# A recurrence in two chains of eight images in place of one chain of sixteen

## The chip, the cores and the metric

The kernel runs on one core of a Trainium2 chip. Its engines are PE (TensorE: matmuls, with its weight loads shown apart as PEld), DVE (VectorE), ACT (ScalarE), POOL (GpSimd) and SP (SyncE, which issues the DMAs). Each has its own stream of instructions, and they meet at semaphores. The metric is the time of one execution on the device in microseconds. Before the change it is 4371.48 us, the median of 3 runs (4370.07 to 4373.3).

## What is computed

The input x has 16 images of 64 channels and 36 x 100 pixels, f32. Four layers follow, each on a normalised x and added to x: sweeps of convolutions, a routed feed-forward layer, sweeps again, and last a recurrence over the 3600 pixels of an image. Only the last layer is touched:

```python
def _L1_ffn_ref(x, W, V, gamma, beta):        # x: (16, 3600, 64) tokens
    Wx = jnp.einsum('bti,hi->bth', x, W)      # then batch norm with gamma, beta
    ...
    Vt = V.T
    def step(yt, wx_t):
        yt = jax.nn.sigmoid(wx_t + yt @ Vt)
        return (yt, yt)
    y0 = jnp.zeros((B, H), dtype=Wx.dtype)
    _, ys = jax.lax.scan(step, y0, jnp.swapaxes(Wx, 0, 1))
    return jnp.swapaxes(ys, 0, 1)
```

Each of the 3600 steps needs the result of the one before. The 16 images don't depend on one another.

## The kernel before

The earlier stages take the first 2475 us or so: norms, which multiply blocks of 400 tokens (L560, L568), sweeps of convolutions, where PE works through L742 and L764, and the routed layer. The last norm leaves the normalised tokens of all images in the buffer `img`. From there the recurrence runs to the end, and every engine has its own loop for it.

The 3600 steps are cut into segments of SEG = 30 steps, and BODY = 4 segments make one iteration of the loops of ACT, DVE and SP (NIT = 30 of them). PE's loop takes 2 segments at a time, 60 iterations. PSUM holds the input part (wx_t) of a segment, 16 columns a step, in bank s for segments of kind s (even or odd).

- PE, for each step (L921 to L944): it waits until the last sigmoid has been counted in `step_y`, multiplies the state before (`yb`, 65 rows, 16 columns) by `vt` in two matmuls of 32 outputs each (L932), adding to what the bank holds, and counts in `step_mm`. In the first 12 steps of a segment it then makes one twelfth of the next segment's input part, `fill_input` (L822 to L829), two matmuls of 40 columns from a staged buffer, and multiplies 512 columns of zeros (`keep_clock`, L832). In the other 18 steps it multiplies 512 and 256 columns of zeros. An f32 matmul stands in the trace as two weight loads and two matmuls. At a segment's first step it also counts in `seg_done`, in every second one it clears `step_y`, and it waits for `staged`.
- ACT, for each step (L1141 to L1146): it waits for `step_mm`, applies the sigmoid to 16 columns of PSUM and writes them to `yb`, and counts in `step_y`. At a segment's first step it also waits for `added`; every 120 steps it clears `step_mm`.
- DVE (L1416), once a segment: it adds the segment's results to the tokens of x2 that SP has loaded into `x2b`, into `ob`.
- POOL (L472), once a segment: it copies the tokens of the segment after next into a staged buffer.
- SP (L450 to L454), once per 4 segments: it loads `x2b` and stores `ob`, 480 KB each, in runs of 480 bytes.

Order is fixed by each engine's program alone; nothing is scheduled. The semaphore waits of PE and ACT are constants, which is why the counters are cleared.

## Time and profile before

| | us |
|---|---|
| median of 3 runs | 4371.48 |
| the profiled execution | 4369.35 |
| its span in the trace | 4367.6 |
| PE busy in the span | 4235.1 (97%) |
| PEld busy | 2684.2 (61%) |
| ACT busy | 1477.0 (34%) |
| DVE busy | 1321.1 (30%) |

The page cuts the span into 40 slices of 109 us. From slice 23 on PE is busy, PEld and ACT at three tenths each, DVE nearly idle, the DMAs at 18 GB/s or less: that is the recurrence, 43% of the span. Busy time of PE counts the multiplied zeros of `keep_clock` as well. In the timeline an entry is a run of like instructions: when it began, how long it lasted, engine, line, operands, how many, and in brackets how long the engine had been idle before it and whom it waited for. Times in the answers are from the start of the span.

### The profile page before, as it was taken

How to read it: one execution, taken by the hardware profiler on the slowest of the kernel's cores; microseconds unless marked ns; L12 is line 12 of the kernel's file. 1: busy time of each engine (PE TensorE's matmuls, PEld its weight loads, DVE VectorE, ACT ScalarE, POOL GpSimd, SP SyncE). 2: the span in 40 equal slices, each digit the busy share in tenths (PEclk: the TensorE clock that was granted, in tenths of full speed). 3: DMA queues.
4: the chain of work that ended last, by engine and by line, in shares of the span. 5: the costliest groups of instructions: out<-in, count | busy, mean ns of one | idle time of the engine just before them, and what ended most of it. 6: DMA issues, size and time to landing. Idle time of an engine off the chain costs nothing.

```text
span 4367.6 us, 106368 instructions
## 1 busy us (share of the span) xinstructions
PE 4235.1 (97%) x42882; PEld 2684.2 (61%) x42882; DVE 1321.1 (30%) x2468; ACT 1477.0 (34%) x5372; POOL 109.2 (3%) x182
## 2 busy tenths in 40 slices
PE   7999999999889999999998899999999999999999
PEld 2799999994352899999993333333333333333333
DVE  3555533334555655533335500000000000000000
ACT  5002344335545002333444233333333333333333
POOL 1000000000010000000000000000000000000000
PEclk8899999999999999999999899999999999999999
DMA  5000000003348000000007200000000000000000
GB/s 138 15 0 0 0 0 0 0 0 108 97 115 254 16 0 0 0 0 0 0 0 200 66 18 10 17 18 18 9 18 18 18 9 18 18 18 9 18 18 14
DMA packets 146888, 139.19 MB, mean 32 GB/s; under 512 B 79710, under 2 KB 146302, under 8 KB 146814
## 3 DMA queue, kind: packets, MB, share of 16 engines
q1 hardware_dynamic: 146814, 138.21, 12.3%
q8 instruction: 46, 0.75, 0.1%
q14 instruction: 28, 0.23, 0.0%
HBM read 79.19 MB, written 58.98 MB: 32 GB/s over the span
## 4 chain that ended last, share of the span: by engine, by line
PE 94%; DVE 3%; ACT 1%; issue 1%; SPq 0%; DMA 0%; DVEq 0%; ACTq 0%; PEldq 0%
PE ps L832 23%; PE ps L764 21%; PE ps L742 18%; PE ps L932 17%; PE ps L827 3%; PE ps L568 2%; PE ps L560 1%; PE ps L715 1%; PE ps L579 1%; PE ps L589 1%; PE ps L603 1%; DVE rstd L1160 1%; PE ps L805 1%; PE ps L682 1%; PE ps L633 1%
## 5 line engine op out<-in xcount | busy, mean ns | idle before, releaser
L832 PE MATMUL ps<-idle 128*32 128x512 bf16 (+1 forms) x5894 | 1635.0, 339 | 0.0
L932 PEld LDWEIGHTS ps<-xl,vt 65*32 65x32 f32 x14400 | 520.9, 108 | 1163.3 <-ACT xl L1146 1111.3
L1146 ACT ACTIVATE xl<-ps 64x16 f32<-64x16 f32 x3600 | 637.2, 177 | 1250.9 <-PE ps L932 1250.9
L764 PE MATMUL ps<-xl,taps 128*128 128x128 f32 (+2 forms) x7880 | 921.5, 279 | 4.7 <-DVE xl L1332 4.7
L764 PEld LDWEIGHTS ps<-xl,taps 128*128 128x128 f32 x7880 | 920.8, 191 | 5.7 <-issue 5.3
L932 PE MATMUL ps<-xl,vt 65*32 65x16 f32 x14400 | 871.2, 193 | 7.8
L742 PE MATMUL ps<-split 128*128 128x400 f32 x4140 | 781.3, 352 | 12.8 <-DVE split L1327 12.8
L742 PEld LDWEIGHTS ps<-split 128*128 128x128 f32 x4140 | 779.2, 190 | 16.6 <-issue 15.2
L1416 DVE TENSOR_TENSOR xl<-xl 64x480 f32<-64x480 f32 x120 | 116.5, 971 | 1772.9 <-PEq L929 886.7
L1002 ACT ACTIVATE img<-xl 128x144 f32 x788 | 366.0, 465 | 556.4 <-DVE xl L1309 556.4
L1309 DVE SCALAR_TENSOR_TENSOR xl<-ps,img 128x144 f32<-128x144 f32 x788 | 323.2, 410 | 597.2 <-PE ps L764 597.2
L832 PEld LDWEIGHTS ps<-idle 128*32 128x32 bf16 x5894 | 426.8, 97 | 21.9 <-issue 10.2
L827 PE MATMUL ps<-xl 128*32 128x40 f32 x5808 | 357.1, 204 | 0.3 <-DVE vt L1408 0.3
L968 ACT ACTIVATE xl<-img 64x400 f32 (+1 forms) x68 | 36.6, 539 | 654.6 <-DVE split L1280 654.6
L1294 DVE SCALAR_TENSOR_TENSOR split<-ps,img 128x400 fp32r<-128x400 f32 x276 | 158.5, 574 | 298.9 <-PE ps L742 298.9
L827 PEld LDWEIGHTS ps<-xl 128*32 128x32 f32 x5808 | 219.1, 112 | 0.5 <-DVE vt L1408 0.5
L1280 DVE TENSOR_TENSOR split<-img,split 128x400 fp32r<-128x400 f32 x280 | 161.1, 575 | 37.9 <-DVE split L1324 1.1
L568 PE MATMUL ps<-rstd,spread 32*128 32x400 f32 x576 | 145.5, 582 | 15.9 <-DVE rstd L1160 14.4
L1296 DVE SCALAR_TENSOR_TENSOR img<-ps,img 128x400 f32 x276 | 155.7, 564 | 0.0
L472 POOL COPY xl<-img 128x240 f32 (+1 forms) x121 | 73.9, 612 | 2942.9 <-PE ps L827 1779.0
L568 PEld LDWEIGHTS ps<-rstd,spread 32*128 32x128 f32 x576 | 53.3, 194 | 106.0 <-issue 32.6
L1051 ACT ACTIVATE taps<-ps 128x400 f32<-128x400 f32 x144 | 72.8, 506 | 114.7 <-PE ps L604 74.5
(153 smaller groups left out, 1681.1 us busy)
## 6 DMA issues: line engine op xcount, KB each, us to landing
ring<-in_x_dram SPq DMA_DIRECT2D x144, 200.0 KB, 3.7
x_dram<-sums SPq DMA_DIRECT2D x144, 200.0 KB, 3.3
t_dram<-sums SPq DMA_DIRECT2D x72, 200.0 KB, 3.6
ring<-t_dram SPq DMA_DIRECT2D x72, 200.0 KB, 3.9
ring<-x_dram SPq DMA_DIRECT2D x72, 200.0 KB, 3.7
xl<-x_dram SPq DMA_DIRECT2D x30, 480.0 KB, 6.3
out_dram<-xl SPq DMA_DIRECT2D x30, 480.0 KB, 4.7
img<-in_L_ffn_weight_dram SPq DMA_DIRECT2D x4, 512.0 KB
```

The costliest lines, as they stand in the source:

```text
L568: pe.matmul(PS[bank][:, 0:CH], spread32[32 * q:32 * q + 32, p * 64:p * 64 + 128], rstd[32 * q:32 * q + 32, (g % 2) * CH:(g % 2 + 1) * CH], ...
L742: ins = pe.matmul(acc[:, :, j0:j1], taps_part[tap_part][:, t0:t0 + 128], line_pairs(h, line_part, j0 + d, j1 + d), start=(tap_part == line ...
L764: last = pe.matmul(acc[:, :, lo:hi], taps[:, (k * NO + d + 2) * 128:(k * NO + d + 3) * 128], column[h][:, :, lo + d:hi + d], start=(n == 0 ...
L827: last = pe.matmul(acc[c * 32:(c + 1) * 32, t0:t0 + FILL_T, h * HB:(h + 1) * HB], wsc[1 - h][:, c * 32:(c + 1) * 32], stage[j][:, t0:t0 + ...
L832: pe.matmul(PS[bank][0:32, 0:n], idle[:, 0:32], idle[:, 0:n], start=True, stop=True)
L932: last = pe.matmul(PS[s][c * 32:(c + 1) * 32, t * B:(t + 1) * B], vt[:, c * 32:(c + 1) * 32], prev, start=False, stop=True, skip_group_che ...
L1002: act.activation(column_at(l, h, x), column[h], ACT.Copy).then_inc(put_back[l][h], 1)
L1146: act.activation(yb[0:64, s % 2, :, t], PS[s % 2][0:64, t * B:(t + 1) * B], ACT.Sigmoid).then_inc(step_y, 1)
L1280: dve.tensor_tensor(line_pairs(h, 1), line, line_pairs(h, 0), ALU.subtract).then_inc(lo[l][h], 1)
L1294: dve.scalar_tensor_tensor(out=line_pairs(h, 0), in0=acc, scalar=0.0, in1=line, op0=ALU.max, op1=ALU.add).then_inc(hi[l][h], 1)
L1296: dve.scalar_tensor_tensor(out=line, in0=acc, scalar=0.0, in1=line, op0=ALU.max, op1=ALU.add).then_inc(state[l][h], 1)
L1309: dve.scalar_tensor_tensor(out=column[h], in0=acc, scalar=0.0, in1=column_at(l, h, x), op0=ALU.max, op1=ALU.add).then_inc(state[l][h], 1)
```

## The change

The 16 images become two groups of eight, h = 0 and 1, each a chain of its own with its own counters, `step_y[h][j]` and `step_mm[h][j]`, j for segments of even and odd number. A chain's counter of one kind is cleared at the first step of a segment of the other kind. In each step PE does chain 0's two matmuls (8 columns), then a part of `fill_input` in the first 8 steps of a segment or 256 columns of zeros in the others, then chain 1's two matmuls, then 256 columns of zeros. ACT does two sigmoids of 8 columns. Each chain has its banks: 2s + h, and the zeros go to bank 4. SEG becomes 20: 180 segments, of which PE's loop still takes 2 (90 iterations) and the loops of ACT, DVE and SP 4 (45 iterations, transfers of 320 KB in runs of 320 bytes).

```diff
-SEG = 30
+SEG = 20
...
-            pool.memset(yb[0:64, 1, :, SEG - 1], 0.0).then_inc(step_y, 2 * SEG)
+            for h in range(2):
+                alone(pool.memset(yb[0:64, 1, h * HB:(h + 1) * HB, SEG - 1], 0.0))
+                pool.sem_inc(step_y[h][1], SEG)
...
-            acc = PS[j][0:64, 0:SEG * B].rearrange("p (t b) -> p t b", b=B)
+            acc = PS[2 * j + h][0:64, 0:SEG * HB].rearrange("p (t b) -> p t b", b=HB)
             for c in range(2):
-                last = pe.matmul(acc[c * 32:(c + 1) * 32, t0:t0 + FILL_T, h * HB:(h + 1) * HB], wsc[1 - h][:, c * 32:(c + 1) * 32],
-                                 stage[j][:, t0:t0 + FILL_T, :], start=(part == 0), stop=True, skip_group_check=True)
+                last = pe.matmul(acc[c * 32:(c + 1) * 32, t0:t0 + FILL_T, :], wsc[1 - h][:, c * 32:(c + 1) * 32],
+                                 stage[j][:, t0:t0 + FILL_T, :], start=(t0 == 0), stop=True, skip_group_check=True)
...
-                        n = s * SEG + t
-                        if n == 0:
-                            pe.wait_ge(step_y, 2 * SEG)
-                            pe.sem_clear(step_y)
-                        else:
-                            pe.wait_ge(step_y, n)
-                        if t == 0:
-                            pe.sem_inc(seg_done, 1)
-                        prev = yb[:, s, :, t - 1] if t else yb[:, 1 - s, :, SEG - 1]
-                        for c in range(2):
-                            last = pe.matmul(PS[s][c * 32:(c + 1) * 32, t * B:(t + 1) * B], vt[:, c * 32:(c + 1) * 32],
-                                             prev, start=False, stop=True, skip_group_check=True)
-                        last.then_inc(step_mm, 1)
-                        if t < 2 * FILLS:
+                        for h in range(2):
+                            pe.wait_ge(step_y[h][s] if t else step_y[h][1 - s], t if t else SEG)
+                            images = slice(h * HB, (h + 1) * HB)
+                            prev = yb[:, s, images, t - 1] if t else yb[:, 1 - s, images, SEG - 1]
+                            for c in range(2):
+                                last = pe.matmul(PS[2 * s + h][c * 32:(c + 1) * 32, t * HB:(t + 1) * HB], vt[:, c * 32:(c + 1) * 32],
+                                                 prev, start=False, stop=True, skip_group_check=True)
+                            last.then_inc(step_mm[h][s], 1)
                             if t == 0:
-                                pe.wait_ge(staged, i * 2 + (s + 2))
-                            last = fill_input(pe, 1 - s, t)
-                            if t == 2 * FILLS - 1:
-                                last.then_inc(filled, 1)
-                            keep_clock(pe, 512)
-                        else:
-                            keep_clock(pe, 512)
-                            keep_clock(pe, 256)
+                                pe.sem_clear(step_y[h][1 - s])
+                                if h == 1:
+                                    pe.sem_inc(seg_done, 1)
+                            if h == 0 and t < 2 * FILLS:
+                                if t == 0:
+                                    pe.wait_ge(staged, i * 2 + (s + 2))
+                                last = fill_input(pe, 1 - s, t)
+                                if t == 2 * FILLS - 1:
+                                    last.then_inc(filled, 1)
+                            else:
+                                keep_clock(pe, 256, 4)
...
-                        n = s * SEG + t
-                        act.wait_ge(step_mm, n + 1)
-                        if n == BODY * SEG - 1:
-                            act.sem_clear(step_mm)
-                        act.activation(yb[0:64, s % 2, :, t], PS[s % 2][0:64, t * B:(t + 1) * B], ACT.Sigmoid).then_inc(step_y, 1)
+                        for h in range(2):
+                            act.wait_ge(step_mm[h][s % 2], t + 1)
+                            act.activation(yb[0:64, s % 2, h * HB:(h + 1) * HB, t], PS[s % 2 * 2 + h][0:64, t * HB:(t + 1) * HB], ACT.Sigmoid
+                                           ).then_inc(step_y[h][s % 2], 1)
+                            if t == 0:
+                                act.sem_clear(step_mm[h][1 - s % 2])
```

The rest of the diff makes room for the added semaphores: in the routed layer and the setup, counters that were counted one after another become one (`ffn_tr`, `ffn_taken`, `rnn_w_ready`), with the same waits in the same places.

The order of PE's instructions around a segment boundary in the middle of its loop. L932 (in the new kernel L930) are the matmuls of a step, L827 (L830) those of the input part, L832 (L835) the zeros, ISA the clear. Before:

```order
L932 MATMUL ps<-xl,vt 32x16
L832 MATMUL ps<-idle 32x512
L832 MATMUL ps<-idle 32x256
L932 MATMUL ps<-xl,vt 32x16 [waits step_y]
L932 MATMUL ps<-xl,vt 32x16
L937 REGISTER_ALU
L827 MATMUL ps<-xl 32x5x8 [waits staged]
L827 MATMUL ps<-xl 32x5x8
L832 MATMUL ps<-idle 32x512
```

Now:

```order
L930 MATMUL ps<-xl,vt 32x8 [waits step_y0_0]
L930 MATMUL ps<-xl,vt 32x8
L934 ISA
L939 REGISTER_ALU
L830 MATMUL ps<-xl 32x40 [waits staged]
L830 MATMUL ps<-xl 32x40
L930 MATMUL ps<-xl,vt 32x8 [waits step_y1_0]
L930 MATMUL ps<-xl,vt 32x8
L934 ISA
L835 MATMUL ps<-idle 32x256
```

The clear, the register instruction, the wait for `staged` and the input matmuls now stand between the two chains' matmuls, and the second clear between chain 1's matmuls and its zeros.

The end of PE's loop, where it jumps back. Before:

```order
L932 MATMUL ps<-xl,vt 32x16 [waits step_y]
L932 MATMUL ps<-xl,vt 32x16
L832 MATMUL ps<-idle 32x512
L832 MATMUL ps<-idle 32x256
L919 REGISTER_ALU
L919 COMPARE_AND_BRANCH
```

Now:

```order
L930 MATMUL ps<-xl,vt 32x8 [waits step_y0_1]
L930 MATMUL ps<-xl,vt 32x8
L835 MATMUL ps<-idle 32x256
L930 MATMUL ps<-xl,vt 32x8 [waits step_y1_1]
L930 MATMUL ps<-xl,vt 32x8
L835 MATMUL ps<-idle 32x256
L922 REGISTER_ALU
L922 COMPARE_AND_BRANCH
```

The jump follows on chain 1's matmuls, and what comes behind it is the first step of chain 0.

ACT at a segment boundary, L1146 (now L1145) the sigmoid. Before:

```order
L1146 ACTIVATE xl<-ps 64x16 [waits step_mm] x29
L1140 REGISTER_ALU
L1146 ACTIVATE xl<-ps 64x16 [waits step_mm,added]
```

Now:

```order
L1145 ACTIVATE xl<-ps 64x8 [waits step_mm1_0]
L1141 REGISTER_ALU
L1145 ACTIVATE xl<-ps 64x8 [waits step_mm0_1,added]
L1148 ISA
L1145 ACTIVATE xl<-ps 64x8 [waits step_mm1_1]
L1148 ISA
L1145 ACTIVATE xl<-ps 64x8 [waits step_mm0_1]
```

A clear now follows each chain's first sigmoid of a segment.

## Rows read from the trace of the kernel before

**Rows 1.** Groups by shape, 2477.5 to 4361: count, busy us, mean ns, idle before
```profile
L832 PE MATMUL ps<-idle 128*32 128x512 bf16 x3597 | 1361.6, 379 | 0.0
...
L1146 ACT ACTIVATE xl<-ps 64x16 f32<-64x16 f32 x3595 | 636.4, 177 | 1247.2 <-PE ps L932 1247.2
L832 PE MATMUL ps<-idle 128*32 128x256 bf16 x2159 | 583.0, 270 | 0.0
L932 PEld LDWEIGHTS ps<-xl,vt 65*32 65x32 f32 x14380 | 519.8, 108 | 1162.3 <-ACT xl L1146 1110.3 <-issue 52.0
```
**Rows 2.** Windows: length, busy us and count by engine, granted clock, DMA share, GB/s
```profile
2477.50:4361.00 1883.50, 1875.67 (x25884) 721.21 (x25880) 115.52 (x119) 636.35 (x3595) 72.23 (x118) 1.00 0.07 15
...
1040.00:1070.00 30.00, 24.37 (x213) 17.82 (x215) 19.81 (x20) 16.13 (x26) 3.19 (x1) 0.89 0.00 1
```
**Rows 3.** Timeline of an ordinary step: start, length, what, idle before
```profile
3000.53 0.18 ACT L1146 ACTIVATE xl<-ps 64x16 f32<-64x16 f32 x1 [0.34 <-PE ps L932]
3000.76 0.14 PEld L932 LDWEIGHTS ps<-xl,vt 65*32 65x32 f32 x4 [0.34 <-ACT xl L1146]
...
3000.84 0.48 PE L832 MATMUL ps<-idle 128*32 128x512 bf16 x2
3001.05 0.18 ACT L1146 ACTIVATE xl<-ps 64x16 f32<-64x16 f32 x1 [0.34 <-PE ps L932]
```
**Rows 4.** Timeline, a segment's second step and the next boundary (inside PE's loop)
```profile
2601.87 0.18 ACT L1146 ACTIVATE xl<-ps 64x16 f32<-64x16 f32 x1 [0.34 <-PE ps L932]
...
2616.38 0.18 ACT L1146 ACTIVATE xl<-ps 64x16 f32<-64x16 f32 x1 [0.34 <-PE ps L932]
2616.67 0.17 PEld L932 LDWEIGHTS ps<-xl,vt 65*32 65x32 f32 x4 [0.40 <-issue]
...
2616.84 0.15 PEld L827 LDWEIGHTS ps<-xl 128*32 128x32 f32 x4
...
2617.04 0.18 ACT L1146 ACTIVATE xl<-ps 64x16 f32<-64x16 f32 x1 [0.48 <-PE ps L932]
```
**Rows 5.** Line L1146 alone: count, ns min/median/max, first and last start
```profile
L1146 ACT ACTIVATE xl<-ps x3600: 177/177/178, 2475.2 to 4361.3; 64x16 f32<-64x16 f32 x190
```
**Rows 6.** Timeline of the boundary where PE's and ACT's loops turn
```profile
2600.07 0.18 ACT L1146 ACTIVATE xl<-ps 64x16 f32<-64x16 f32 x1 [0.34 <-PE ps L932]
...
2600.67 0.18 ACT L1146 ACTIVATE xl<-ps 64x16 f32<-64x16 f32 x1 [0.43 <-PE ps L932]
...
2601.00 0.15 PEld L932 LDWEIGHTS ps<-xl,vt 65*32 65x32 f32 x4 [0.52 <-issue]
...
2601.35 0.18 ACT L1146 ACTIVATE xl<-ps 64x16 f32<-64x16 f32 x1 [0.50 <-PE ps L932]
```
**Rows 7.** Lines L1051, L932 and L568 alone, as in rows 5
```profile
L1051 ACT ACTIVATE taps<-ps x144: 503/503/514, 1003.6 to 2439.9; 128x400 f32<-128x400 f32 x144
...
L932 PE MATMUL ps<-xl,vt x14400: 176/183/236, 2474.8 to 4360.9; 65*32 65x16 f32 x198
...
L568 PE MATMUL ps<-rstd,spread x576: 494/598/1032, 46.6 to 2460.6; 32*128 32x400 f32 x192
```
**Rows 8.** Timeline of a step with input matmuls
```profile
3010.24 0.14 PEld L932 LDWEIGHTS ps<-xl,vt 65*32 65x32 f32 x4 [0.28 <-ACT xl L1146]
...
3010.30 0.15 PEld L827 LDWEIGHTS ps<-xl 128*32 128x32 f32 x4
...
3010.40 0.38 PE L832 MATMUL ps<-idle 128*32 128x512 bf16 x1
```
**Rows 9.** Timeline, the last add
```profile
4361.56 0.96 DVE L1416 TENSOR_TENSOR xl<-xl 64x480 f32<-64x480 f32 x1 [14.81 <-PEq L946]
```
**Rows 10.** Timeline, the loop's first steps, granted clock still at the lower level
```profile
2475.18 0.18 ACT L1146 ACTIVATE xl<-ps 64x16 f32<-64x16 f32 x1 [1.89 <-PE ps L932]
...
2475.79 0.18 ACT L1146 ACTIVATE xl<-ps 64x16 f32<-64x16 f32 x1 [0.43 <-PE ps L932]
...
2476.45 0.18 ACT L1146 ACTIVATE xl<-ps 64x16 f32<-64x16 f32 x1 [0.49 <-PE ps L932]
```

More of the change, by code:

```diff
@@ L120, in metaformer @@
         yb = xl[0:65, 0:2 * SEG * B].rearrange("p (s t b) -> p s b t", s=2, b=B)
-        x2b = xl[0:64, 1920:3840].rearrange("p (b t) -> p b t", b=B)
-        ob = xl[0:64, 3840:5760].rearrange("p (b t) -> p b t", b=B)
+        x2b = xl[0:64, 1920:1920 + BODY * SEG * B].rearrange("p (b t) -> p b t", b=B)
+        ob = xl[0:64, 3840:3840 + BODY * SEG * B].rearrange("p (b t) -> p b t", b=B)
         wsc = [xl[:, 5760 + h * 64:5824 + h * 64] for h in range(2)]
@@ L164, in __init__ @@
                     self.summed = sem(f"ln{n}_summed")
+                if n in (1, 2):
                     self.mixed = sem(f"ln{n}_mixed")
@@ L192, in metaformer @@
         xt_tr, xt_kept = sem("xt_tr"), sem("xt_kept")
-        hid_tr, hid_turned, eo_kept, eo_tr = (sem(n) for n in ("hid_tr", "hid_turned", "eo_kept", "eo_tr"))
+        ffn_tr, ffn_taken = sem("ffn_tr"), sem("ffn_taken")
         ew_dma, hid_mm, hid_act, eo_mm, outt_ready, lh_tr, lh_ready = (
@@ L197, in metaformer @@
             sem(n) for n in ("rdma", "rnn_t", "rnn_w_ready", "bn_pe", "bn_dve", "bn_step", "rnn_ready"))
-        bn_std, rnn_t_taken, rnn_c = sem("bn_std"), sem("rnn_t_taken"), sem("rnn_c")
+        bn_std, rnn_c = sem("bn_std"), sem("rnn_c")
         pool_done, taps_blank = sem("pool_done"), sem("taps_blank")
         passed = sem("passed")
-        step_mm, step_y, seg_done, x2_in, added, out_st = (
-            sem(n) for n in ("step_mm", "step_y", "seg_done", "x2_in", "added", "out_st"))
+        step_mm, step_y = ([[sem(f"{n}{h}_{j}") for j in range(2)] for h in range(2)] for n in ("step_mm", "step_y"))
+        seg_done, x2_in, added, out_st = (sem(n) for n in ("seg_done", "x2_in", "added", "out_st"))
         staged, filled = sem("staged"), sem("filled")
@@ L846, in _ @@
             pe.wait_ge(centre_ready, 1)
-            pe.wait_ge(rnn_t_taken, 1)
+            pe.wait_ge(rnn_w_ready, 1)
             for h in range(2):
@@ L875, in _ @@
                     last = pe.transpose(PS[4 + j][:, u * 128:(u + 1) * 128], hidden[:, j * 512 + u * 128:j * 512 + (u + 1) * 128], ident[:, :])
-                last.then_inc(hid_tr, 1)
+                last.then_inc(ffn_tr, 1)
             for part in range(2):
@@ L881, in _ @@
             for j in range(4):
-                pe.wait_ge(hid_turned, j + 1)
+                pe.wait_ge(ffn_taken, j + 1)
                 for e8 in (2 * j, 2 * j + 1):
@@ L889, in _ @@
             last.then_inc(eo_mm, 1)
-            pe.wait_ge(eo_kept, 1)
+            pe.wait_ge(ffn_taken, 5)
             for e8 in range(8):
@@ L893, in _ @@
                 if e8 % 4 == 3:
-                    last.then_inc(eo_tr, 1)
+                    last.then_inc(ffn_tr, 1)
             pe.wait_ge(outt_ready, 2)
@@ L900, in _ @@
             pe_layer(pe, 1)
-            pe.wait_ge(rnn_w_ready, 1)
+            pe.wait_ge(rnn_w_ready, 2)
             pe_token_norm(pe, 3)
@@ L945, in _ @@
-            pe.wait_ge(step_y, 2 * SEG)
+                        for h in range(2):
[6 more added lines that the diff above has]
+                            last.then_inc(step_mm[h][s], 1)
+                            if t == 0:
+                                pe.sem_clear(step_y[h][1 - s])
[9 more added lines that the diff above has]
+                                keep_clock(pe, 256, 4)
@@ L946, in _ @@
+            for h in range(2):
+                pe.wait_ge(step_y[h][1], SEG)
             pe.sem_inc(seg_done, 1)
@@ L1141, in _ @@
                     for t in range(SEG):
-                        n = s * SEG + t
-                        act.wait_ge(step_mm, n + 1)
-                        if n == BODY * SEG - 1:
-                            act.sem_clear(step_mm)
-                        act.activation(yb[0:64, s % 2, :, t], PS[s % 2][0:64, t * B:(t + 1) * B], ACT.Sigmoid).then_inc(step_y, 1)
+                        for h in range(2):
+                            act.wait_ge(step_mm[h][s % 2], t + 1)
[3 more added lines that the diff above has]
+                                act.sem_clear(step_mm[h][1 - s % 2])
         def dve_taps(dve, l):
@@ L1359, in _ @@
                 dve.tensor_copy(half(wbd, h)[:, h * 64:(h + 1) * 64], PS[7][0:64, 64:128])
-            dve.tensor_copy(vt[0:64, :], PS[7][0:64, 128:192]).then_inc(rnn_t_taken, 1)
+            dve.tensor_copy(vt[0:64, :], PS[7][0:64, 128:192]).then_inc(rnn_w_ready, 1)
             dve_taps(dve, 0)
@@ L1372, in _ @@
             for j in range(4):
-                dve.wait_ge(hid_tr, j + 1)
-                dve.tensor_copy(hidden_t[:, j * 512:(j + 1) * 512], PS[4 + j][:, :]).then_inc(hid_turned, 1)
+                dve.wait_ge(ffn_tr, j + 1)
+                dve.tensor_copy(hidden_t[:, j * 512:(j + 1) * 512], PS[4 + j][:, :]).then_inc(ffn_taken, 1)
             dve.wait_ge(eo_mm, 1)
-            dve.tensor_copy(mixed_out, PS[0][:, :]).then_inc(eo_kept, 1)
+            dve.tensor_copy(mixed_out, PS[0][:, :]).then_inc(ffn_taken, 1)
             for u in range(2):
-                dve.wait_ge(eo_tr, u + 1)
+                dve.wait_ge(ffn_tr, 5 + u)
                 dve.tensor_copy(outt.rearrange("p (b a x) -> p b a x", a=4, x=8)[:, :, :, 4 * u:4 * u + 4],
```

## The prediction, written before the result was known

> **What bounds the kernel now.** The page's slices and groups point at one loop, from 2477 to 4361 us; I then read its groups by shape, stretches by window, and the timeline of single steps. In the loop stand 14380 small weight loads of L932, 3595 sigmoids of L1146, and the idle matmuls of L832 [rows 1]. TensorE looks full there (1875.67 us busy of 1883.50, at a granted clock of 1.00) [rows 2], but the reader is to see what it is full of: L832 multiplies zeros, to keep the clock up. The loop is a closed chain of 3600 steps, two matmuls then one sigmoid that feeds the next two. The timeline shows one turn of it [rows 3]: the weight load of L932 starts 0.23 us after the sigmoid started (0.18 of it the sigmoid, 0.05 the way back), the next sigmoid starts 0.29 us after that load. ACT's idle gap of 0.34 and PE's of 0.34 are both waits for the other. So the loop is bound by latency, and by no engine's rate.
>
> Its size: from the sigmoid at 2601.87 to that at 2616.38 [rows 4] are 28 steps without a boundary, 14.51/28 = 0.5182 us each. All 3600 sigmoids start between 2475.2 and 4361.3 [rows 5], 1886.1 us. 3599 x 0.5182 is 1865.0, so 21.1 us are extras: 119 segment boundaries of about 0.15 (2616.38 to 2617.04 is 0.66 [rows 4], and 0.67 in the other kind [rows 6], for 0.52), 30 turns of ACT's loop of about 0.08 (2600.07 to 2600.67 is 0.60 [rows 6]), and 0.4 us of steps at the lower clock at the start.
>
> **What two chains can and can't do.** A chain's next step still waits for its own sigmoid, so two chains don't halve the step. Both advance once per turn of one chain, and a turn gets shorter only by what 8 images cost less than 16. Everything else is a question of whether the second chain fits into the gaps of the first.
>
> **Term 1, shorter operations.** The sigmoid reads 16 columns in 177 ns, L1051 reads 400 from PSUM in 503 [rows 7]: (503 - 177)/384 = 0.85 ns a column, so 8 fewer give 6.8 ns. For the matmul the nearest pair is L932's 183 ns for 16 f32 columns and the shortest of L568, 494 ns for 400 [rows 7]: 0.81 ns a column, 6.5 ns for 8. Only the last of the matmuls counts, those before it hide behind the next weight load. Together 13.3 ns, a turn of 0.505 us, and 3600 x 13.3 ns = 47.9 us. The lower bound is the sigmoid's part alone, 24 us; the upper is a matmul part half as long again, 60 us.
> A rule of the Trainium skill speaks against the matmul half. "TensorE: Matmul & The Clock Gate", section "Back-to-back issue gap", says that starts of matmuls never come closer than about 25 ns however few columns they have; by it the term would be 24 us only. No row here has 8 columns, so the trace doesn't decide it; I take the slope because what counts here is the end of one matmul and not the distance between two.
>
> **Term 2, does the second chain fit?** On PE a group (matmuls plus filler) took, in a step with input matmuls, from the load at 3010.24 over that of L827 at 3010.30 to the filler's start at 3010.40 [rows 8], 0.16 us. The new order has that without the filler in chain 0, and in chain 1 (and in both where no input is made) the matmuls, 0.08 us to the filler's start [rows 3], and 256 columns of filler, 0.11 us (a filler of 512 columns is recorded with 379 ns, one of 256 with 270) [rows 1]: 0.19 us. Two groups need 0.35 to 0.38 of 0.505 us, so each chain finds PE free if they stand 0.19 to 0.31 apart. ACT needs 2 x 0.17 = 0.34 of 0.505. I cost ordinary steps at nothing beyond term 1; the cover is 0.12 us a step on PE, and if it is gone the turn grows one for one.
>
> **Term 3, boundaries: 180 for 120.** Before, at a boundary, the load of L932 comes 0.29 after the sigmoid's start instead of 0.23 (the wait and the count of seg_done stand alone in front of it), and the next sigmoid 0.37 after it instead of 0.29 (two waits, `added` too) [rows 4]. In the new order the matmul waits itself and the clear and count come after it, so the 0.06 goes, and some 0.03 of slower loading (0.17 for 0.14, the length of the two load rows [rows 3, 4]); about 0.05 for the second wait on ACT stays. What is new lies between the two chains. On PE the clear, the register instruction and the wait on `staged` stand between chain 0's matmuls and chain 1's: register and wait cost 0.11 (0.17 from load to input load for 0.06 in an ordinary step [rows 4, 8]), the clear about 0.10 (0.33 from sigmoid to load for 0.29 with a plain count, and that 0.06 over none [rows 4, 6]). Chain 1's load can then start 0.06 + 0.11 + 0.10 + 0.06 = 0.33 us after chain 0's; it was due 0.25 after, a delay of 0.08. Chain 1's own clear pushes its filler to end about 0.63, where chain 0 is due at 0.585. ACT's two clears (0.08 each by [rows 6]) stand between sigmoids that are 0.25 apart, with 0.08 to spare, and cost nothing. DVE's add and the pool's copy, for whom the counts of seg_done and filled are, have some 10 us and keep it. In all 0.05 to 0.15 a boundary; I take 0.075, 13.5 us.
>
> **Term 4, PE's loop turns: 90 for 60.** Before, PE jumps while it would wait for the sigmoid anyway. From the last load before the turn (0.23 after 2600.07) to the first behind it (2601.00) are 0.70 us [rows 6], and the jump, the register instructions and a clear fit in there. In the new order the last group is chain 1's, chain 0 is due only about 0.26 us later, and nothing covers the rest. The price is above 0 (if the jump is short) and below 0.70 - 0.26 = 0.44 us a turn. No row shows the jump alone; I take 0.2, the middle: 18 us, with 0 and 40 as ends. The Trainium skill ("Advanced Engine Details and Errata", section "Control Flow Timing") gives about 108 ns for a compare-and-branch and 51 ns for a branch; by that alone the turn would cost nothing or little, and the sum would be some 15 us lower; no row here shows it.
>
> **Term 5, the ends.** From DVE's last add at 4361.56 [rows 9] to the end of the span, 4367.6, it is one add and one store; both shrink by a third in size, and a good part of each is fixed: -1 us. Four input parts fewer ahead of the loop: below 1 us. Merged semaphores of the earlier stages keep the same order of waits: 0. Packets of 320 bytes for 480, in 45 for 30 transfers each way: hidden, since x2's load has a segment (10 us) to land.
>
> **Sum.** Terms 3 and 4 give 31.5 us (9 to 67) in place of 21.1: +10. With -48 and -1 that is -39 us. The profiled execution took 4369.35 us (span 4367.6 and 1.75 around it), 2.1 below the median of 4371.48; on the median's side 4332.5.
>
> **Rivals.**
> (A) The forecast: 4333 us, its own range 4300 to 4362 by the bounds of the terms. 0.55.
> (B) The matmul's part doesn't shrink, or the chains touch by some 7 ns a step: 4371.5 - 24 + 10 - 1 = 4356. For it: PE's loads of 32 columns (0.14 us for four [rows 3]) are as long as before. 0.13.
> (C) Turns and boundaries at their upper ends: 67 for 21.1 is +46, with a gain of 24 to 48 that gives 4369 to 4392. For it: PE's order is now shared, and a late chain passes its lateness on. 0.10.
> (D) The other side: the clock. Zeros are multiplied in 768 columns a step now (512 with input matmuls); then it is 512, and 256 with input matmuls, in a turn that is hardly shorter. Where PE waited more, as at 1040 to 1070, the granted clock falls (0.89, with PE busy 24.37 of 30 us) [rows 2]. At the lower of its two levels, 1.2 GHz, the first steps of this loop took 0.61 and 0.66 us (2475.18, 2475.79, 2476.45) [rows 10] for 0.518: at least 0.09 us a step. All 3600 so would be +324 us, 4657; the input steps alone (8 of 20) +130, 4463. It turns the sign from 39/0.09 = 430 steps on, 12% of them. Against it: the loop now runs at 1.00 for 1883 us with a steady pattern [rows 2], the new pattern has no long gap either, and four weight loads more a step. 0.20, the price anywhere from 4380 to 4660.
> (E) The change doing nothing of what it says is excluded by the order of instructions, which has the two chains; 0.02 for what I don't see.
>
> **How the numbers follow.** The likeliest is 4333. The range must hold A, B and most of C: 4298 (term 1 at 60, terms 3 and 4 low) to 4388 leaves out D and the rest, 0.2. A measurement of this kernel can tell about 0.2% (9 us) from no change: faster, below 4362.7, is A and B, 0.68; within 0.2% is half of C and a little of D, 0.09; slower is the rest, 0.23.
>
> **What would show it.** Sigmoids of 170 ns, in pairs; those of one chain 0.505 apart within a segment, the second about 0.25 behind the first. If 0.512, B. The stretch of the loop at a granted clock of 1.00; anything lower is D and outweighs all other terms. Intervals of 0.58 at boundaries of one chain, and of about 0.8 at every second one, where PE turns; if the latter are 0.6, term 4 was too dear. PE's idle time before L932 should be `issue` at turns only. Wrong in its ground would be an ordinary turn above 0.518, for then the chains hinder each other in every step.

## The result, and the profile after

The changed kernel takes 4342.36 us (median of 4 runs, 4336.4 to 4347.19) against 4370.77 (4368.68 to 4373.3) for the kernel before, measured beside it: a ratio of 0.9933, interval 0.9921 to 0.9945. It is faster by 28.4 us, which is three times what a measurement can tell. The forecast was 4333 with the sign right and 9 us too little. The profiled execution took 4347.19 us (span 4345.4), the slowest of the four. The runs lie in two pairs, about 4347 and about 4337. The account below is that of one run of the slower pair, and the gap of 10 us is taken up in the part on the prediction.

The groups of the loop in the page after (columns as in [rows 1], with the mean over all shapes):

```profile
L930 PE MATMUL ps<-xl,vt 65*32 65x8 f32 x28800 | 1700.5, 187 | 9.5
L1145 ACT ACTIVATE xl<-ps 64x8 f32<-64x8 f32 x7200 | 1224.3, 170 | 638.1 <-PE ps L930 44.7
L930 PEld LDWEIGHTS ps<-xl,vt 65*32 65x32 f32 x28800 | 1059.5, 108 | 627.6 <-ACT xl L1145 26.7
```

There are twice as many sigmoids, each 170 ns for 177, and four weight loads a chain and step. The line L1145 alone answers to [rows 5]:

```profile
L1145 ACT ACTIVATE xl<-ps x7200: 170/170/173, 2479.6 to 4340.5; 64x8 f32<-64x8 f32 x195
```

The sigmoids span 1860.9 us for 1886.1 before: 25.2 us less. What else differs lies outside: the loop begins at 2479.6 for 2475.2, though nothing that costs time was changed ahead of it. In the traces of all fourteen kernels here that point lies between 2470.8 and 2485.3 with the same stages ahead of it, so these 4 us are within its scatter. Behind the last sigmoid stand 4.9 us for 6.3.

An ordinary stretch in the timeline of after (columns as in [rows 3]):

```profile
3000.02 0.14 PEld L930 LDWEIGHTS ps<-xl,vt 65*32 65x32 f32 x4
...
3000.28 0.14 PEld L930 LDWEIGHTS ps<-xl,vt 65*32 65x32 f32 x4
3000.28 0.23 PE L930 MATMUL ps<-xl,vt 65*32 65x8 f32 x4
...
3000.53 0.14 PEld L930 LDWEIGHTS ps<-xl,vt 65*32 65x32 f32 x4
```

One chain loads at 3000.02 and 3000.53, the other at 3000.28, in the middle. And the boundary where PE's loop turns, which answers to [rows 6]:

```profile
3119.85 0.14 PEld L930 LDWEIGHTS ps<-xl,vt 65*32 65x32 f32 x4
...
3120.08 0.14 PEld L930 LDWEIGHTS ps<-xl,vt 65*32 65x32 f32 x4
...
3120.51 0.30 PEld L930 LDWEIGHTS ps<-xl,vt 65*32 65x32 f32 x4 [0.27 <-ACT xl L1145]
...
3120.95 0.17 PEld L930 LDWEIGHTS ps<-xl,vt 65*32 65x32 f32 x4
3120.99 0.22 PE L930 MATMUL ps<-xl,vt 65*32 65x8 f32 x4
3121.00 1.44 ACT L1145 ACTIVATE xl<-ps 64x8 f32<-64x8 f32 x6 [0.47 <-PE ps L930]
```

Chain 0 loaded at 3119.85 and was due at 3120.36; it came at 3120.51, 0.15 late, and its four loads then took 0.30 us in place of 0.14: the first is there, and the second follows 0.16 us later (0.01 in an ordinary step). Both go to the price of the turn. The jump itself is an instruction of PE's sequencer, which the page doesn't count as busy. Both traces have it (count, ns min/median/max, first and last start), before's first:

```profile
L919 PEldq COMPARE_BRANCH  x60: 76/208/208, 2506.1 to 4361.0; - x60
```
```profile
L922 PEldq COMPARE_BRANCH  x90: 76/208/208, 2499.6 to 4340.3; - x90
```

A jump that is taken holds the sequencer for 208 ns; the 76 ns are the last one, which is not. Here it starts at 3120.18, 0.32 us ahead of the first load behind it. The name of the releaser is not to be trusted here: chain 0's sigmoid had ended in time for 3120.36.

**The loop as an account.** From the starts of all sigmoids of chain 0 (each interval to the next, medians by kind; the step is the interval inside a segment) each trace gives the same few numbers. The table has the kernels of the experiments too, named by their labels. The last column is what all other steps took over the median: in before and one_chain_seg20 mostly ACT's loop turns (30 or 45 of 0.08 us), in the others slow steps.

| kernel | step | plain boundary | boundary where PE turns | rest, inside segments |
|---|---|---|---|---|
| before | 0.518 | 0.660 | 0.674 | 4.1 us |
| after | 0.505 | 0.565 | 0.865 | 5.4 us |
| one_chain_seg20 | 0.518 | 0.660 | 0.836 | 5.6 us |
| two_chains_seg30 | 0.505 | 0.565 | 0.737 | 0.2 us |
| zeros_352 | 0.505 | 0.565 | 0.878 | 0.4 us |
| chain0_alone | 0.505 | 0.566 | 0.609 | 11.8 us |
| added_by_pe | 0.505 | 0.505 | 0.980 | 13.1 us |
| seg30_zeros_352 | 0.505 | 0.565 | 0.738 | 0.4 us |
| seg30_352_added_by_pe | 0.505 | 0.505 | 0.702 | 4.5 us |

For after: 3599 x 0.505 = 1817.5 us, boundaries 90 x 0.060 + 89 x 0.36 = 37.4 us (37.8 by the single values), 5.4 us of slow steps, 1860.7 in all. For before: 1864.3 and 21.8 us of boundaries and loop turns, 1886.1.

**The clock.** Three windows of after: the loop, a stretch at the full clock and one of the low ones behind a turn (columns as in [rows 2]):

```profile
2485.00:4330.00 1845.00, 1835.28 (x39959) 1208.18 (x39957) 123.92 (x178) 1213.60 (x7138) 82.91 (x177) 0.99 0.07 16
3137.50:3144.33 6.83, 6.71 (x145) 4.29 (x143) 0.70 (x1) 4.30 (x26) 0.00 (x0) 1.00 0.02 5
3144.33:3151.16 6.83, 6.83 (x131) 5.68 (x129) 0.00 (x0) 4.04 (x24) 0.47 (x1) 0.50 0.40 91
```

In nine stretches of 3.4 or 6.8 us, 41 us in all, the granted clock was 0.50 (the 1.2 GHz level); steps there took 0.553 us where input is made and 0.587 in most others. Each begins 2.3 to 3.7 us after a jump of PE's loop, though most jumps (80 of 89) have none behind them.

### The profile page after: what moved, and what is told of

It is laid out like the page before. It is cut to its first block, busy times and chain, and to the rows that moved or that the text cites. A ratio compares the mean times of both kernels' runs of the same rounds, so it can differ in the third digit from the quotient of the medians.

```text
span 4345.4 us, 140208 instructions
## 1 busy us (share of the span) xinstructions
PE 4210.0 (97%) x57266; PEld 3180.3 (73%) x57266; DVE 1330.6 (31%) x2528; ACT 2064.1 (48%) x8972; POOL 119.5 (3%) x243
## 4 chain that ended last, share of the span: by engine, by line
PE 94%; DVE 3%; issue 1%; ACT 1%; SPq 1%; DMA 0%; DVEq 0%; ACTq 0%; PEldq 0%
PE ps L930 23%; PE ps L767 21%; PE ps L745 18%; PE ps L835 16%; PE ps L830 4%; PE ps L571 3%; PE ps L563 1%; PE ps L582 1%; PE ps L592 1%; PE ps L718 1%; PE ps L606 1%; DVE rstd L1162 1%; PE ps L808 1%; PE ps L636 1%; PE ps L685 1%
## 5 line engine op out<-in xcount | busy, mean ns | idle before, releaser
L930 PE MATMUL ps<-xl,vt 65*32 65x8 f32 x28800 | 1700.5, 187 | 9.5
L1145 ACT ACTIVATE xl<-ps 64x8 f32<-64x8 f32 x7200 | 1224.3, 170 | 638.1 <-PE ps L930 44.7
L930 PEld LDWEIGHTS ps<-xl,vt 65*32 65x32 f32 x28800 | 1059.5, 108 | 627.6 <-ACT xl L1145 26.7
L835 PE MATMUL ps<-idle 128*32 128x256 bf16 (+1 forms) x5894 | 1516.7, 275 | 0.0
L1418 DVE TENSOR_TENSOR xl<-xl 64x320 f32<-64x320 f32 x180 | 125.3, 696 | 1738.1 <-PEq L934 1728.7
L835 PEld LDWEIGHTS ps<-idle 128*32 128x32 bf16 x5894 | 586.9, 100 | 23.2 <-issue 12.4
L830 PE MATMUL ps<-xl 128*32 128x40 f32 x5792 | 359.7, 206 | 0.5 <-DVE vt L1410 0.3
L830 PEld LDWEIGHTS ps<-xl 128*32 128x32 f32 x5792 | 219.8, 112 | 14.9 <-DVE vt L1410 0.5
L473 POOL COPY xl<-img 128x160 f32 (+1 forms) x181 | 84.6, 468 | 2924.3 <-PE ps L830 1756.7
```

What stands on the lines that cost most here:

```text
L830: last = pe.matmul(acc[c * 32:(c + 1) * 32, t0:t0 + FILL_T, :], wsc[1 - h][:, c * 32:(c + 1) * 32], stage[j][:, t0:t0 + FILL_T, :], start= ...
L835: pe.matmul(PS[bank][0:32, 0:n], idle[:, 0:32], idle[:, 0:n], start=True, stop=True)
L930: last = pe.matmul(PS[2 * s + h][c * 32:(c + 1) * 32, t * HB:(t + 1) * HB], vt[:, c * 32:(c + 1) * 32], prev, start=False, stop=True, skip ...
L1145: act.activation(yb[0:64, s % 2, h * HB:(h + 1) * HB, t], PS[s % 2 * 2 + h][0:64, t * HB:(t + 1) * HB], ACT.Sigmoid).then_inc(step_y[h][s ...
```

## Experiments

Twelve kernels ran, each beside the kernel before. The theory after the result: the step is shorter by the operations' own lengths, the second chain costs nothing in it, and the rest is given back where PE jumps. Rivals: the chains slow one another, or the shorter segment costs by its count of boundaries and not by the jump.

### The two parts of the change apart

`one_chain_seg20`: the kernel before with segments of 20 steps.

```diff
-SEG = 30
+SEG = 20
```

> The kernel before with SEG = 20 only: one chain of sixteen, 180 boundaries, 45 turns of ACT's loop, 90 of PE's. Theory (the gain is term 1, the shorter operations of the chains; PE's loop turn is hidden while one chain waits for its sigmoid): a step stays 0.518 us, a boundary costs 0.15 over it in both kinds, so the extras grow from 21 to about 31 us and the time is about 4379 us, 9 above the kernel before. Rival (short segments are themselves worth something, as smaller transfers and adds): 4370 or below. Second rival (PE's turn is dear whatever runs in the loop): boundaries with a turn at 0.9 us instead of 0.67, and over 4395 us.

Measured 4397.46 us (4396.55 to 4400.27), ratio 1.0054 (1.0040 to 1.0067): 23 us more where some 9 were expected. Its plain boundaries are 0.660 as before, so 60 more of them cost what was thought. But the boundary where PE turns grew from 0.674 to 0.836, so the second rival, a dear turn whatever runs in the loop, came nearest. The jump is covered: the first load behind it starts 0.32 us after the sigmoid, as in before. The second load isn't: it follows 0.18 us later, and 0.01 in before. PE's loads had waited 52.0 us on `issue` before [rows 1]; here:

```profile
L932 PEld LDWEIGHTS ps<-xl,vt 65*32 65x32 f32 x13934 | 513.6, 108 | 1138.0 <-ACT xl L1146 1055.6 <-issue 76.3
```

`two_chains_seg30`: the changed kernel with segments of 30.

```diff
-SEG = 20
+SEG = 30
```

> The changed kernel with SEG = 30: two chains, 60 turns of PE's loop and 60 other boundaries instead of 90 and 90. Theory (a turn costs chain 0 0.36 us over a step of 0.505, another boundary 0.06): 30 x 0.36 + 30 x 0.06 = 12.6 us less than the changed kernel, about 4330 us. Rival (the turn's cost grows with the length of the loop's body, which is fetched anew): no gain, 4340 or more.

Measured 4331.07 us (4318.45 to 4332.74), ratio 0.9902 (0.9887 to 0.9917), 11 us less than the changed kernel. That is the expected number, but by luck, as two things that weren't expected cancel. The profiled run is the fastest of the four, 4318.45 us: its boundaries cost 17.3 us for 37.8, so 20 us less and not 12.6, since a turn is 0.737 us for 0.865, and no step is slow. The other three took 4329 to 4333 us at a mean granted clock of 0.978 for 0.985. That is 61 us more at the lower level, some 8 us by what such stretches cost in after (5.4 us in 41), an estimate; no trace of them was kept. The turn in the timeline of the profiled run:

```profile
3422.71 0.14 PEld L930 LDWEIGHTS ps<-xl,vt 65*32 65x32 f32 x4
...
3422.94 0.14 PEld L930 LDWEIGHTS ps<-xl,vt 65*32 65x32 f32 x4
...
3423.36 0.17 PEld L930 LDWEIGHTS ps<-xl,vt 65*32 65x32 f32 x4 [0.27 <-ACT xl L1145]
```

Chain 0 is due at 3423.22 and comes 0.15 late, as in after; but its loads take 0.17 and not 0.30. So with two chains both ways of cutting have the jump's 0.15, and segments of 20 have 0.13 us more than segments of 30 between the first weight load behind the jump and the second; with one chain of 16 they have 0.16 more. The shorter segment is a loss twice over: 30 more turns, and each dearer.

### The second chain left out

`chain0_alone`: in PE's and ACT's loops h runs over 0 only, and of chain 1's group only the 256 columns of zeros are left. Images 8 to 15 are not computed.

```diff
-                        for h in range(2):
+                        for h in range(1):
```

> Chain 1 is left out (images 8 to 15 are not computed, and each step has a second filler of 256 columns so that PE's clock stays up); chain 0 is as in the changed kernel. Theory (the chains don't touch within a segment, and what the second one costs is the loop turn, which a single chain covers with its wait for the sigmoid, and a little at boundaries): step 0.505, plain boundaries 0.05 to 0.06 over it, turns 0.06 to 0.12 over it in place of 0.36; about 23 us below the changed kernel, 4318. Rival (the chains cost each other something in each step): step 0.500 or less. Rival (the turn's cost is not covered in any case): turns at 0.36 and 4340.

Measured 4331.84 us (4329.05 to 4334.54), ratio 0.9903 (0.9888 to 0.9918), where 4318 was expected. The step is 0.505 with the second chain and without: the chains don't hinder one another in a step, and a chain of eight is what sets 0.505. The difference is at the turn, 0.609 for 0.865. The first load behind the jump is on time, and the second comes 0.06 us after it, though the segments have 20 steps. Alone, the jump lies behind chain 0's own matmuls, which leave it time until the sigmoid is done; with chain 1 it lies 0.23 us later. Of the 14 us by which this kernel missed its expectation the clock had most: 29 stretches at the lower level, 113 us, with 10 of the 11.8 us of longer steps in and beside them. The window 2490 to 4300 has

```profile
2490.00:4300.00 1810.00, 1631.52 (x25440) 729.19 (x25438) 122.89 (x177) 605.88 (x3532) 83.21 (x177) 0.97 0.07 16
```

### How often PE turns

`pe_turns_45`: PE's loop over four segments instead of two, so 45 turns for 90.

```diff
-            with pe.Fori(0, NIT * BODY // 2) as i:
-                for s in range(2):
+            with pe.Fori(0, NIT) as i:
+                for part in range(BODY):
+                    s = part % 2
...
-                                    pe.wait_ge(staged, i * 2 + (s + 2))
+                                    pe.wait_ge(staged, i * BODY + (part + 2))
```

> The changed kernel with four segments in a turn of PE's loop in place of two, so 45 turns instead of 90; all else the same. Theory: each turn replaced by a plain boundary saves 0.36 - 0.06 = 0.30 us, 13.5 us in all, about 4329 us; the remaining turns still cost 0.36. Rival (what costs is the segment boundary of the odd kind, not the jump): the intervals of 0.865 us stay at 90 and the time stays at 4342.

Measured 4688.2 us (4681.22 to 4696.67), ratio 1.0722 (1.0707 to 1.0736): the largest miss of the study. Its timeline at a turn, and the instruction queue on the two pages (after's second):

```profile
3985.63 0.14 PEld L931 LDWEIGHTS ps<-xl,vt 65*32 65x32 f32 x4
...
3990.70 0.13 PEld L931 LDWEIGHTS ps<-xl,vt 65*32 65x32 f32 x1 [4.91 <-issue]
...
3993.79 0.18 PEld L931 LDWEIGHTS ps<-xl,vt 65*32 65x32 f32 x3 [2.97 <-issue]
...
3994.17 0.17 ACT L1146 ACTIVATE xl<-ps 64x8 f32<-64x8 f32 x1 [8.09 <-PE ps L931]
```
```profile
q8 instruction: 490, 8.03, 0.8%
```
```profile
q8 instruction: 46, 0.75, 0.1%
```

PE stands 4.9 us, issues one load, and stands another 3.0. In 44 turns the instruction queue moved 444 packets of 16.4 KB more, ten a turn. The loop's body has 1807 PE instructions in the trace (weight loads, matmuls and the sequencer's own), against 905 in after and 1353 in `two_chains_seg30`, whose turns show nothing of the kind and whose page has no such packets. So somewhere between 1353 and 1807 the body no longer stays in the engine's store and is loaded again each time round. The Trainium skill ("Runtime: NRT & Kernel Launch", section "Instruction fetch mechanics") says that PE holds 2048 instructions, refilled in blocks of 16 KiB. The packets agree in size. The limit of 2048 no run here shows: 1807 is below it, and whether the edges of blocks or instructions that the trace doesn't record make up the rest is open. Behind the waits the clock fell as well, to 0.87 over 2490 to 4300. Of the 343 us by which the loop is longer than that of after, 313 are boundaries (351 for 38) and 29 slow steps.

### The zeros, and the rival of the clock

Three kernels change only the width of the filler in a step (for `zeros_352`; the others alike):

```diff
-                                keep_clock(pe, 256, 4)
+                                keep_clock(pe, 352, 4)
```

`zeros_128`. 

> The changed kernel with 128 columns of zeros in a filler in place of 256: the price of rival D. Theory (the granted clock follows what PE has to do, and 256 is near the edge, since the changed kernel's trace shows nine stretches of 3.4 to 6.8 us at the lower level in this loop): the clock is at 1.2 GHz for much or all of the loop, steps there take 0.55 to 0.60 us, and the time is 4450 to 4700 us. Rival (the dips are only what the pause at a loop turn does): as many dips as with 256 columns, step 0.505, 4335 to 4350 us.

`zeros_352`. 

> The changed kernel with 352 columns of zeros in a filler in place of 256. Theory (the granted clock falls now and then because PE does less; PE has 0.12 us a step to spare, of which 96 columns more in one or two fillers take 0.04 to 0.08): step still 0.505, granted clock 1.00 throughout the loop, about 5 us less than the profiled execution of the changed kernel and runs that agree within 3 us, 4334 to 4338. Rival (the dips come from elsewhere): as many dips, 4336 to 4347 as before. Second rival (the chains touch): step above 0.505, slower.

`zeros_512`. 

> The changed kernel with 512 columns of zeros in a filler: the cover of term 2 used up. Theory (a group of PE is 0.08 us to the filler's start plus 0.21 us for 512 columns, 0.30 us; two of them 0.60, over a step of 0.505; with input matmuls in place of one filler 0.46, under it): 12 of 20 steps take 0.60 us, 8 stay at 0.505, about 205 us more, 4547 us. Rival (the weight loads of a waiting group go ahead of the zeros, so that a group is shorter): steps of 0.52 to 0.56 and under 4450.

The windows 2490 to 4300 of the three, in this order:

```profile
2490.00:4300.00 1810.00, 1805.25 (x35990) 1465.77 (x35989) 111.82 (x161) 1094.27 (x6428) 75.09 (x161) 0.50 0.07 15
```
```profile
2490.00:4300.00 1810.00, 1804.04 (x39290) 1177.40 (x39285) 122.19 (x175) 1199.88 (x7018) 82.92 (x176) 1.00 0.07 16
```
```profile
2490.00:4300.00 1810.00, 1809.17 (x37306) 1290.37 (x37301) 115.68 (x166) 1133.47 (x6662) 78.52 (x167) 1.00 0.07 15
```

With 128 columns the whole loop runs at the lower level: 4512.52 us, ratio 1.0313 (1.0297 to 1.0329), a step of 0.553. This is the state that rival (D) of the prediction spoke of, at a price of 0.048 us a step. With the changed kernel's 256 columns it is dearer: in the stretches of after a step with input matmuls is 0.048 over 0.505 and most others 0.082, by 8 and 12 of 20 steps 0.068 (an estimate), against the 0.09 that [rows 10] gave for one chain of 16 columns with 768 columns of zeros. With 352 columns no step is slow: 4340.31 (4339.1 to 4343.5), ratio 0.9924 (0.9910 to 0.9937), and the runs lie within 4.4 us. The median gains 2 us, less than can be told from nothing and less than the 5 expected; turns became 0.013 us dearer (89 x 0.013 = 1.2 us). With 512 columns 4445.36 (4440.19 to 4445.74), ratio 1.0163 (1.0147 to 1.0178): the filler (0.38 us) and the matmuls no longer fit where no input is made, and steps take 0.550 there and 0.505 in most others. Two groups so cost 0.55 and not the 0.60 of the two lengths added; that weight loads run ahead of the zeros, as the rival had it, fits the number and wasn't tested by itself. The cover in term 2 is real, and it ends between 352 and 512 columns.

### The bookkeeping at a boundary

`bookkeeping_moved`: PE's clears, its count and its wait for `staged` stand at steps 1 and 2 in place of fillers, the input parts at steps 2 to 9, ACT's clears at step 15.

```diff
-                            if t == 0:
-                                pe.sem_clear(step_y[h][1 - s])
-                                if h == 1:
+                            if h == 1 and t in (1, 2):
+                                pe.sem_clear(step_y[t - 1][1 - s])
+                                if t == 1:
...
+                            elif h == 0 and t == 1:
+                                pe.wait_ge(staged, i * 2 + (s + 2))
+                                keep_clock(pe, 64, 4)
```

> The changed kernel with PE's clears, the register instruction, the wait on staged and the count of seg_done moved from a segment's first step to its second and third, where they stand in place of a filler, the input parts to steps 2 to 9, and ACT's clears to step 15. Theory (at a plain boundary chain 0 pays 0.06 us for ACT's second wait, which stays, and PE's work is in its shade): no more than 2 us gained, 4340 to 4342, boundaries still 0.565. Rival (PE's clear and register instruction are on the path, as term 3 had it): up to 180 x 0.03, 5 us gained.

Measured 4459.35 us (4456.29 to 4470.53), ratio 1.0198 (1.0183 to 1.0213), at a granted clock of 0.74 over 2490 to 4300. Plain boundaries stayed 0.565 and turns 0.87, so none of the moved instructions had been what they cost. The slow steps, 120 us over 0.505 each, lie in the stretches at the lower level or at their edges. The loss is the clock's, as the same kernel with 352 columns shows:

`moved_zeros_352`. 

> The kernel with the bookkeeping moved (4459.35 us, half of the loop at the 1.2 GHz level) with fillers of 352 columns in place of 256. Theory: its loss was the clock alone, which it lost since the steps beside a boundary have fewer zeros there; with wider fillers the clock stays up, steps are 0.505 us and the boundaries of chain 0 stay 0.565 us: 4338 to 4342 us. Rival: the moved instructions themselves cost (the wait for staged and the clears between the chains): then steps away from the boundary are 0.505 us, but those beside it are late, and the time is over 4350 us at a full clock.

Measured 4346.84 us (4336.29 to 4351.14), ratio 0.9942 (0.9921 to 0.9962), clock 0.99. All but 4.5 us of the loss against the changed kernel are back, and 7.5 us of slow steps, more than after's 5.4, stand in the profiled run. That leaves the plain boundary's 0.060 us. At the head of a segment ACT waits twice before chain 0's sigmoid, for `step_mm` and for `added`. The trace of after has one of the two waits as an instruction of its own, once a segment:

```profile
L1144 ACTq EVENT_SEMAPHORE  x180: 17/17/17, 2479.5 to 4330.6; - x180
```

It is the one for `step_mm`, which ends last, and the sigmoid, which itself waits for `added`, starts 0.062 us after it. That can be tested, if PE takes the wait for `added` over, with the register instruction that goes with it: ACT's later sigmoids follow PE's matmuls anyway.

`added_by_pe`:

```diff
-                    act.wait_ge(added, i * BODY + (s + 1))
...
+                            elif h == 0 and t == 2 * FILLS + 2:
+                                pe.wait_ge(added, i * 2 + (s + 2))
+                                keep_clock(pe, 64, 4)
```

> The changed kernel with one wait moved: ScalarE no longer waits for the semaphore added at the head of a segment, where two waits stand before chain 0's first sigmoid. TensorE waits for it instead, in step 10 of the segment before, in front of a filler (shortened there to 64 columns); that ScalarE's later sigmoids come after it follows from the matmuls that they wait for. Theory: the 60 ns by which chain 0 is late at an ordinary segment boundary (sigmoid to sigmoid 0.565 us for 0.505) are a second wait instruction on ScalarE between the matmul's end and the sigmoid; then the boundary falls to 0.505 to 0.52 us and the loop turn of TensorE from 0.865 to about 0.81, 180 x 0.055 = 10 us less in all: about 4332 us. Rival: the 60 ns come from TensorE's side (clear, banks, the first matmul of a segment), and then the boundary stays 0.565 us and the time 4336 to 4347.

Measured 4356.76 us (4354.71 to 4360.86), ratio 0.9969 (0.9956 to 0.9981). The cause is shown: ACT's separate wait is gone from the trace, and all 90 plain boundaries of chain 0 are 0.505 us, as long as a step. But the time went up, by 14 us. The turn is now 0.980 for 0.865:

```profile
3122.79 0.11 PEld L930 LDWEIGHTS ps<-xl,vt 65*32 65x32 f32 x1 [0.27 <-ACT xl L1148]
3122.82 0.47 PE L930 MATMUL ps<-xl,vt 65*32 65x8 f32 x4
3123.06 0.14 PEld L930 LDWEIGHTS ps<-xl,vt 65*32 65x32 f32 x3 [0.17 <-issue]
```

The second load behind the jump comes 0.27 us after the first. And the clock fell in 17 stretches, 89 us in all. Of the 13.1 us of slow steps 11.4 lie there; the rest is mostly the first step of a segment, at the full clock. The 5.4 us that the plain boundaries gave were paid for with 8.2 us at the turns and 7.7 of slow steps more than in after.

### The best of them together

`seg30_zeros_352`. 

> The changed kernel with segments of 30 steps and fillers of 352 columns. The two edits alone gave 4331.07 us (whose runs lay between 4318.45 and 4332.74) and 4340.31 (4339.1 to 4343.5). Theory: the wider filler only keeps the clock from falling for a few us after a loop turn, and the longer segment saves 30 loop turns and 30 ordinary boundaries; so the runs gather at the lower end, 4318 to 4322 us, with a spread under 5 us. Rival: the wider fillers cost at each boundary, where they stand before the first matmul after the jump (0.014 us a turn in the run with 352 columns), or start a collision with the input steps: 4325 us or more.

Measured 4320.32 us (4318.33 to 4322.27), ratio 0.9884 (0.9868 to 0.9901), spread 4 us: the fastest of the study, and 22 us ahead of the changed kernel. In its trace no step after the start is at the lower clock.

`seg30_352_added_by_pe`. 

> All three together: segments of 30 steps, fillers of 352 columns, and the wait for added on TensorE in step 14 of the segment before. If the three act on different terms they add: 4318 to 4322 less 120 x 0.055 = 6.6 us, so 4312 to 4316 us. If the second wait on ScalarE is not what the boundary costs: 4318 to 4322 again.

Measured 4322.46 us (4317.55 to 4329.11), ratio 0.9892 (0.9875 to 0.9908): no gain on top. Boundaries cost 12.3 us for 17.4, but 4.5 us came back in steps of 0.52 to 0.55 at the full clock. Nearly all of that, 4.0 us, is the first step of a segment (118 of 120 are longer than the rest), where PE's clears, its count and its wait for `staged` stand; the step with the wait for `added`, step 14, is not longer than others. Chain 1 had stood 0.23 us behind chain 0; here it stands 0.28 behind. Whether that is what makes those instructions count now wasn't tested.

## Why the prediction came out as it did

- **Term 1, -47.9 us: right.** The step is 0.505 us, the loop's steps 46.8 us shorter. The sigmoid is 170 ns for 177; the matmul half is there in full: of 13 ns a step 7 are the sigmoid's, and from a group's last weight load to its sigmoid's start are 0.249 us for 0.255. The Trainium skill's rule of about 25 ns ("TensorE: Matmul & The Clock Gate", section "Back-to-back issue gap") was set against this half: it is a floor for the distance between starts of matmuls, and the step shows no such floor. `chain0_alone` has the same step, so it belongs to the eight columns. Rival (B) is out.
- **Term 2, 0: right.** With and without the second chain the step is the same, and the cover can be spent up to 352 columns but not to 512. Chain 1 stands 0.23 to 0.26 behind chain 0, as said.
- **Term 3, 0.075 a boundary: right in kind, a bit dear.** It measured 0.060, and its cause is the one named, the second wait on ACT; without it the boundary is a step. What was put between the chains (clears, wait for `staged`) cost chain 0 nothing, and the 0.08 by which chain 1 was to be late beside it didn't show: its sigmoid stands 0.23 us behind chain 0's at the head of a segment as elsewhere.
- **Term 4, 0.2 a turn: the term that was mis-sized.** A turn costs 0.30 us over a plain boundary (0.865 - 0.565), 89 x 0.10 = 9 us more than taken. The jump's own lateness was 0.15, inside the bounds and near the middle chosen. What the step left out is that the instructions behind the jump's target come late as well: 0.15 us of it between the first weight load and the second, as much as the jump. The trace of before couldn't show it, for its turns don't have it (0.674 for 0.660, and 0.01 us between the two loads); that it comes with segments of 20 steps, with one chain of 16 (0.18) as with two (0.16) and hardly with one chain of eight (0.06), is measured, and not why. The jump alone it did show, though the rows chosen don't: a taken branch is 208 ns in before as in after. The Trainium skill ("Advanced Engine Details and Errata", section "Control Flow Timing") gives about 108 ns for a compare-and-branch; the trace doesn't agree, and the measurement decides. The jump and what follows it cost 0.31 us of lateness. A turn at no cost, which the prediction drew from that page, would have put this term 27 us too low.
- Terms 3 and 4 together: 37.8 us for 31.5 expected, within the 9 to 67 that were given, so rival (C) had its place but not its price.
- **Rival (D), 0.20: right in mechanism, small in size.** The clock fell, behind the turns, in 41 of 1861 us, 5.4 us in the profiled run. The price of a slow step was near the 0.09 taken (0.048 to 0.082), but few steps had it. I had asked only whether the ordinary pattern would hold the clock. That the change stands near the edge is shown on both sides: 352 columns, none (though 7.5 us where the bookkeeping is moved as well); 256 columns with one step in twenty at 320 columns in all for 512, 11 us (`added_by_pe`), and with two steps at 64 and at none for 256, 120 us (`bookkeeping_moved`); 128 columns, all of it. The 10 us between the runs of after are its in part at most: the mean granted clock (0.98 in the slower pair, 0.983 in the faster) is some 30 us more at the lower level, 4 us by what such a stretch costs in the loop (an estimate). No trace of the faster pair was kept, and the start of the loop alone scatters by 14 us; the rest is open.
- **Sum.** -46.8 + 37.8 - 21.8 + 5.4 = -25.4 us in the loop, -1.4 behind it (forecast -1), and +4.4 ahead of it from scatter; the profiled executions differ by 22.2, the medians by 28.4. Of the 16 us between the forecast's -38.5 and the -22.2 of the profiled executions, terms 3 and 4 have 6.3, the clock 5.4, the scatter 4.4. That the median came 6 us nearer to the forecast is no merit of its terms.

What would have given the 9 us of term 4: reading the turn as "jump, then the instructions behind it", with the second part unknown and its upper end open.

## What to carry to other kernels

Where a loop is bound by the latency of one chain, a second chain in its gaps costs nothing in the step as long as both groups fit with room to spare; the gain is only what the smaller operations cost less. It takes away cover elsewhere, though: a jump that hid behind the one chain's wait comes to lie on the path, so look at the loop turns first and cut fewer of them (30-step segments gave 11 us, with wider fillers 22), up to the body size at which the loop is fetched anew. With 30-step segments and the old fillers three of four runs had a lower mean clock and 11 us more than the fourth, so the two edits belong together. And where filler work keeps the clock up, taking away a wait or a filler has to be paid for in filler elsewhere.

## What the runs showed of the hardware that was not expected

- **A body too long for the store.** A body of 1353 recorded PE instructions turns in 0.23 us over a plain step, one of 1807 in 7.8 us over it (the interval is 8.3), with ten 16.4 KB packets each time.
- **Behind a jump, the second weight load can be late** by 0.16 us (after), 0.18 (`one_chain_seg20`), 0.06 (`chain0_alone`), 0.03 (30-step segments), 0.27 (`added_by_pe`), counted from the first, with nothing in the program between them; 0.01 is the ordinary distance. Wider fillers add a little (0.13 us with 128 columns, there at the lower clock, 0.17 with 352, 0.20 with 512). `one_chain_seg20` and `chain0_alone` have bodies of equal length (583), so neither that nor the number of chains decides it; it stays open whether the place of the code does.
- **A taken branch at the end of PE's loop takes 208 ns**, one that isn't taken 76, in before and after alike; where the body is loaded anew (`pe_turns_45`) it takes 4.8 us.
- **Two waits in front of one instruction cost 0.06 us** when the one that ends last is the separate one, and nothing when there is only one: 0.565 and 0.505.
- **The lower clock costs a chain of latencies little**: at half the clock 0.553 for 0.505 us a step, 10%, with 128 columns of filler, and 0.587, 16%, in the steps of after with two fillers of 256.
